# Building the tables ahead of a state-space mixing step in another order, with part of the work moved from VectorE to GpSimd

## The chip, the cores and the metric

The kernel runs on one core of a Trainium2 chip, in a single launch. The metric is device time in microseconds: the median of several executions. Profiles are taken from one execution.

## What is computed

The program is one layer of a tower: a diagonal state-space kernel as token mixer, then attention, then a gated low-rank feed-forward part. The change lies in the first part, which is:

```python
dt = exp(log_dt)                        # H = 256
w = -exp(log_w_real) + 1j * w_imag      # (256, 64)
dtA = w * dt[:, None]
Cm = Cc * (exp(dtA) - 1.0) / w          # Cc: 8 x 256 x 64, complex, the input x
h = 2 * real(einsum('chn,hnl->chl', Cm, exp(dtA[:, :, None] * arange(512))))
# h (8, 256, 512) then goes through
h = h + attention(layernorm(h), w_q, w_k, w_v, w_o)   # 16 heads, 4 kv heads, window 256
h = h + gated_lora_ffn(layernorm(h), ...)             # 8 experts, argmax gate
```

## The kernel before, in words

The 512 positions l are written as l = e0 + 8 e1 + 64 e2 with three digits of 0 to 7. So exp(dtA l) is a product of three small complex factors, one for each level k = 0, 1, 2, and each is a magnitude exp(rho·level) times a cosine and a sine. `mag[:, k]`, `ang[:, k]` and `rnd[:, k]` hold 128 x (128 x 8) values for a level. Level 0 becomes the table v, level 1 the table u, and level 2 the table P (`ptab`). The factor d = (exp(dtA) - 1)/w is multiplied into P; this gives `pa` and its turned copy `pb`.

Four engines build the tables, and each follows its own written-out program with semaphores:

- ScalarE (`trig`, lines 771 to 791): magnitudes of all 24 digits, then for each level sine, absolute value and cosine. Level 0 goes to PSUM (`v_trig`, in `bank_quad`), level 1 to `utab`, level 2 to `ptab`. Between levels 0 and 1 it makes `sin1`, `half` and `cos1`, which d needs. It then splits two weight chunks, and makes from v the rotated v (`vrot`), the edges of b, the copies `lefts`, and `turn_p`, which writes `pb`.
- VectorE: rho (link 16 of its chain, `CH_RHO`), the turns, `reduce_angles` for three levels (a rounding and a subtraction each), the reciprocal of |w|^2, `expm1_parts` with the result `em1`, the u table (`times_mag`, line 1096), d (lines 1101 to 1115), the v table (line 1117), and `p_times_d` (lines 1127 to 1130), which waits for P times its magnitude (`p_mag`). `link` makes each next instruction wait for the one before; instructions without it follow in the pipeline.
- GpSimd: |w|^2 (lines 584 to 589), then P times its magnitude in two halves (line 596), but only after a wait for `d_poles`, and for the second half of the poles three instructions of P times d (605 to 608). Then come the 16 steps of the mixing (`chunk`, lines 570 and 575).
- TensorE: five matmuls to warm up (line 1573) once v is done (`v_done`), then 16 steps of 128 small matmuls (line 1559), each waiting for VectorE (`b_ready`, `g1_ready`), ScalarE (`edges`) and GpSimd (`g2_ready`).

dr, ndr and ndi are slices of `dd` and hold the real part, its negative and the negated imaginary part of d. `d_first` and `d_rest` are copies of them in PSUM. `mw` is exp(log_w_real), kept in `ex`, and `wim` is the imaginary part of w.

Of the kernel before, what the change touches and what calls it, by code (L numbers as in the profile page):

```python
# [21 lines left out]
ALU = mybir.AluOpType  # L22
# [3 lines left out]
P = 128  # L26
# [13 lines left out]
LE = 8  # L40
TYPES = 3
NQ = 16
# [6 lines left out]
ROUND = 1.5 * 2.0 ** 23  # L49
# [27 lines left out]


CH_RHO = 16

GATE, GATE_Z, GATE_KEEP = 15, 7, 11

# [66 lines left out]
def tower(nc, mix_c, mix_s, log_dt, log_wr, w_im, w_qkv, w_o, w_gate, w_gmul, w_upd, centers, slopes, consts, out):  # L149
# [3 lines left out]
    with top:  # L153
        def sem(name):
            return top.enter_context(nc.semaphore(name))

        def sb(name, shape, dt=F32, stack=top):
            return stack.enter_context(nc.sbuf_tensor(name, shape, dt))
# [9 lines left out]
        v_trig = quad[:].rearrange("p k e -> p (k e)").rearrange("p (q r e) -> p q r e", q=NQ, r=2)  # L168
# [22 lines left out]
        vtab = sb("vtab", [P, NQ, 2, 64], F32, mixer)  # L191
        vrot = sb("vrot", [P, NQ, 2, 64], F32, mixer)
        utab = sb("utab", [P, NQ, 2, 64], F32, mixer)
# [6 lines left out]
        mag = sb("mag", [P, TYPES, P, LE], F32, early)  # L200
# [15 lines left out]
        ang = sb("ang", [P, TYPES, P, LE], F32, small)  # L216
        rnd = sb("rnd", [P, TYPES, P, LE], F32, small)
# [6 lines left out]
        wim = sb("wim", [P, P], F32, scratch)  # L224
        rho = sb("rho", [P, P], F32, scratch)
        turn = sb("turn", [P, P], F32, scratch)
        em1 = sb("em1", [P, P], F32, scratch)
        sin1 = sb("sin1", [P, P], F32, scratch)
# [3 lines left out]
        ai = sb("ai", [P, P], F32, scratch)  # L232
        dd = sb("dd", [P, 3, P], F32, scratch)
        ndi, ndr, dr = (dd[:, k, :] for k in range(3))
# [97 lines left out]
        def raw_turn(n):  # L332
# [7 lines left out]
        chain, nrm_parts, nrm_sum = sem("dve_chain"), sem("nrm_parts"), sem("nrm_sum")  # L340
        mag_ready, ang_ready, trig_ready = sem("mag_ready"), sem("angles_ready"), sem("trig_ready")
        abs_done, v_done, u_done, rot_done = sem("abs_done"), sem("v_table"), sem("u_table"), sem("rotated_v")
        wim_in, d_poles, pa_pool, pool_prod, p_mag, p_prod, pa_done, pb_done = (
            sem("wim_in"), sem("d_of_poles"), sem("pa_of_pool"), sem("pool_products"), sem("p_times_mag"), sem("p_products"), sem("pa_ready"), sem("pb_ready"))
        left_ready, t2_done = sem("left_ready"), sem("t2_done")
        b_ready, edges, g1_ready, g2_ready, mixed, evac, xd_out = (
            sem("b_ready"), sem("b_edges"), sem("g1_ready"), sem("g2_ready"), sem("mixed_ready"), sem("evacuated"),
# [208 lines left out]
        def _(pool):  # L556
# [24 lines left out]
            mw = ex[:, 1, :]  # L581
            pool.wait_ge(chain, CH_RHO)
            pool.wait_ge(wim_in, 16)
# [3 lines left out]
            nc.gpsimd.tensor_tensor(nrm[:], nrm[:], wsq[:], ALU.add).then_inc(nrm_parts, 1)  # L587
            pool.wait_ge(nrm_parts, 2)
            nc.gpsimd.tensor_scalar(nrm[:], nrm[:], 0.5, 1.0, ALU.mult, ALU.mult).then_inc(nrm_sum, 1)
            pool.wait_ge(d_poles, 1)  # L590
            pool.wait_ge(trig_ready, 4)
            for k in range(2):
                qs = slice(k * HALF_Q, (k + 1) * HALF_Q)
                m = mag[:, 2].rearrange("p (q h) e -> p q (h e)", q=NQ)[:, qs].unsqueeze(2).to_broadcast(
                    [P, HALF_Q, 2, 64])
                nc.gpsimd.tensor_tensor(ptab[:, qs], ptab[:, qs], m, ALU.mult).then_inc(p_mag, 1)

            def per_pole(t):
                return t[:, HALF_Q * QH8:].rearrange("p (q h) -> p q h", q=HALF_Q).unsqueeze(3).to_broadcast(
                    [P, HALF_Q, QH8, LE])  # L600

            second = slice(HALF_Q, NQ)
            grid = lambda t: t.rearrange("p q (h e) -> p q h e", h=QH8)
            pool.wait_ge(p_mag, 2)
            nc.gpsimd.tensor_tensor(grid(pq[2][:]), grid(ptab[:, second, 0, :]), per_pole(dr), ALU.mult)
            nc.gpsimd.tensor_tensor(grid(pq[3][:]), grid(ptab[:, second, 1, :]), per_pole(ndi), ALU.mult).then_inc(pool_prod, 1)
            pool.wait_ge(pool_prod, 1)
# [142 lines left out]
        def _(act):  # L750
# [11 lines left out]
            levels = [e * LE ** k for k in range(TYPES) for e in range(LE)]  # L762
            act.wait_ge(chain, CH_RHO)
            for k in range(TYPES):
# [111 lines left out]
            def swap(s, parts=range(3), keys=7):  # L876

                for j in parts:
                    view, _, _, _ = rope_view(j)
                    act.wait_ge(proj, s * 3 + (j + 1))  # L880
                    if j == 0 and (not isinstance(s, int) or s):
                        act.wait_ge(kq_rot, s * 3)
                    src = banks[keys][:, 0:S] if j == 0 else banks[j][:].rearrange("p (h s) -> p h s", h=2)
                    nc.scalar.activation(view(sw)[0:64], src[64:128], ACT.Copy)  # L884
                    nc.scalar.activation(view(sw)[64:128], src[0:64], ACT.Copy).then_inc(swapped, 1)  # L885
# [149 lines left out]
        def _(dve):  # L1035
            links = [0]

            def link(ins):

                links[0] += 1  # L1040
                ins.then_inc(chain, 1)
                dve.wait_ge(chain, links[0])

            v = nc.vector

            def expm1_parts(xin, n, raw_in):

                k, r, q, p2 = (t[:].rearrange("p a b -> p (a b)")[:, 0:n] for t in (kk, rr, qq, ki))
                link(v.tensor_scalar(xin, raw_in, -87.0, 88.0, ALU.max, ALU.min))
                link(v.tensor_scalar(k, xin, 1.4426950408889634, ROUND, ALU.mult, ALU.add))  # L1050
                link(v.tensor_scalar(k, k, ROUND, None, ALU.subtract))
                link(v.scalar_tensor_tensor(r, k, -0.693359375, xin, ALU.mult, ALU.add))
                link(v.scalar_tensor_tensor(r, k, 2.12194440e-4, r, ALU.mult, ALU.add))
                link(v.tensor_scalar(q, r, 1.0 / 5040, None, ALU.mult))
                for c in (1.0 / 720, 1.0 / 120, 1.0 / 24, 1.0 / 6, 0.5, 1.0):
                    link(v.scalar_tensor_tensor(q, q, c, r, ALU.add, ALU.mult))
                link(v.tensor_scalar(p2, k, 127.0, 8388608.0, ALU.add, ALU.mult))
                return q, p2.bitcast(F32)
# [3 lines left out]
            q, p2 = expm1_parts(flat, 2 * P, flat)  # L1062
# [3 lines left out]
            dt, mw = ex[:, 0, :], ex[:, 1, :]  # L1066
            link(v.scalar_tensor_tensor(rho[:], mw, -1.0, dt, ALU.mult, ALU.mult))
            assert links[0] == CH_RHO, links
            dve.wait_ge(wim_in, 16)
# [5 lines left out]
            def reduce_angles(k, src):  # L1075

                step = ROUND / LE ** k
                link(v.tensor_scalar(flat(rnd[:, k]), flat(src), step, step, ALU.add, ALU.subtract))
                v.tensor_tensor(flat(ang[:, k]), flat(src), flat(rnd[:, k]), ALU.subtract).then_inc(ang_ready, 1)
                dve.wait_ge(ang_ready, k + 1)  # L1080
# [2 lines left out]
            lv = cst[:, C_L:C_L + LE]  # L1083
            link(v.tensor_tensor(ang[:, 0], turn[:].unsqueeze(2).to_broadcast([P, P, LE]),
                                 lv.unsqueeze(1).to_broadcast([P, P, LE]), ALU.mult))
            for k in range(TYPES):
                reduce_angles(k, ang[:, max(k - 1, 0)])
            dve.wait_ge(nrm_sum, 1)
            link(v.reciprocal(nrm[:], nrm[:]))
            q, p2 = expm1_parts(t0[:], P, rho[:])  # L1090
# [3 lines left out]
            def times_mag(tab, k):  # L1094
                m = mag[:, k].rearrange("p (q h) e -> p q (h e)", q=NQ).unsqueeze(2).to_broadcast([P, NQ, 2, 64])
                return v.tensor_tensor(tab[:], tab[:], m, ALU.mult)

            dve.wait_ge(mag_ready, 3)
            dve.wait_ge(trig_ready, 3)
            times_mag(utab, 1).then_inc(u_done, 1)  # L1100
            link(v.tensor_tensor(t1[:], half[:], half[:], ALU.mult))
            v.scalar_tensor_tensor(ai[:], em1[:], 1.0, sin1[:], ALU.add, ALU.mult)
            link(v.tensor_tensor(ar[:], em1[:], cos1[:], ALU.mult))
            link(v.scalar_tensor_tensor(ar[:], t1[:], -2.0, ar[:], ALU.mult, ALU.add))
            v.tensor_tensor(dr, ai[:], wim[:], ALU.mult)
            v.tensor_tensor(t1[:], ar[:], mw, ALU.mult)
            v.tensor_tensor(ndi, ai[:], mw, ALU.mult)
            link(v.tensor_tensor(t2[:], ar[:], wim[:], ALU.mult))
            v.tensor_tensor(dr, dr, t1[:], ALU.subtract)
            link(v.tensor_tensor(ndi, ndi, t2[:], ALU.add))  # L1110
            v.tensor_tensor(ndi, ndi, nrm[:], ALU.mult)
# [1 line left out]
            link(v.tensor_tensor(dr, dr, nrm[:], ALU.mult))  # L1113
            v.tensor_copy(d_first, dd[:, :, 0:HALF_Q * QH8]).then_inc(d_poles, 1)
            link(v.tensor_copy(d_rest, dd[:, 0:2, HALF_Q * QH8:]))
            m = mag[:, 0].rearrange("p (q h) e -> p q (h e)", q=NQ).unsqueeze(2).to_broadcast([P, NQ, 2, 64])
            v.tensor_tensor(vtab[:], v_trig, m, ALU.mult).then_inc(v_done, 1)

            other = banks[4].rearrange("p (q e) -> p q e", q=HALF_Q)

# [118 lines left out]
            def rope(s, j, keys=7):  # L1239
                view, table, _, _ = rope_view(j)  # L1240
                src = banks[keys][:, 0:S] if j == 0 else banks[j][:].rearrange("p (h s) -> p h s", h=2)
                dve.wait_ge(swapped, s * 3 + (j + 1))
                v.tensor_tensor(view(kq), src, table(cosT), ALU.mult).then_inc(kq_cos, 1)  # L1243
# [701 lines left out]
```

## Time and profile before

| what | value |
|---|---|
| median of 3 runs | 802.74 us (802.38 to 805.21) |
| profiled execution | 801.88 us, its span in the trace 800.0 us |
| TensorE matmul busy | 736.1 us, 92% |
| VectorE busy | 575.0 us, 72% |
| ScalarE busy | 444.9 us, 56% |
| GpSimd busy | 434.4 us, 54% |
| mean granted TensorE clock | 0.994 of full |

The names PE, DVE, ACT, POOL and SP in the profile stand for TensorE, VectorE, ScalarE, GpSimd and the engine that issues most transfers. Times in the trace are microseconds from the start of the span; a line such as L1096 is a line of the kernel. The tables are built in the first 38 us or so and the mixing ends near 98 us. After that come attention and the feed-forward part, in which TensorE is nearly always busy.

### The profile page before, as it was taken

How to read it: one execution, taken by the hardware profiler on the slowest of the kernel's cores; microseconds unless marked ns; L12 is line 12 of the kernel's file. 1: busy time of each engine (PE TensorE's matmuls, PEld its weight loads, DVE VectorE, ACT ScalarE, POOL GpSimd, SP SyncE). 2: the span in 40 equal slices, each digit the busy share in tenths (PEclk: the TensorE clock that was granted, in tenths of full speed). 3: DMA queues.
4: the chain of work that ended last, by engine and by line, in shares of the span. 5: the costliest groups of instructions: out<-in, count | busy, mean ns of one | idle time of the engine just before them, and what ended most of it. 6: DMA issues, size and time to landing. Idle time of an engine off the chain costs nothing.

```text
span 800.0 us, 19498 instructions
## 1 busy us (share of the span) xinstructions
PE 736.1 (92%) x6902; PEld 671.3 (84%) x6902; DVE 575.0 (72%) x1604; ACT 444.9 (56%) x1236; POOL 434.4 (54%) x649
## 2 busy tenths in 40 slices
PE   0277788999999999999999999999999999999996
PEld 0166768999999999999989999999999998989883
DVE  7999877887765666766674565665666678888886
ACT  6735435665555667555674555555575655465431
POOL 1488866644444747544474564444384745665632
PEclk9999999999999999999999999999999999999999
DMA  9023741100010203000011020000020000000403
GB/s 217 6 56 79 178 138 34 54 8 2 7 47 8 67 8 99 7 7 7 7 29 39 1 93 8 7 7 1 8 68 7 29 8 8 7 7 13 100 1 105
DMA packets 38127, 31.59 MB, mean 39 GB/s; under 512 B 23790, under 2 KB 29294, under 8 KB 38070
## 3 DMA queue, kind: packets, MB, share of 16 engines
q1 hardware_dynamic: 37606, 30.25, 14.3%
q8 instruction: 35, 0.57, 0.3%
q10 hardware_dynamic: 464, 0.59, 0.3%
q14 instruction: 22, 0.18, 0.1%
HBM read 20.34 MB, written 10.49 MB: 39 GB/s over the span
## 4 chain that ended last, share of the span: by engine, by line
PE 81%; DVE 7%; POOL 4%; ACT 3%; issue 2%; DMA 1%; DVEq 0%; SPq 0%; ACTq 0%; POOLq 0%
PE bank_quad L1548 17%; PE bank_quad L1547 16%; PE bank_quad L1549 16%; PE bank_pair L1547 4%; PE bank_pair L1548 4%; PE bank_pair L1549 4%; PE bank_quad L1559 2%; PE bank_pair L1736 2%; PE bank_pair L1746 2%; PE bank_quad L1665 2%; PE bank L1746 2%; PE bank L1750 2%; PE bank L1547 2%; PE bank L1548 2%; PE bank L1549 1%
## 5 line engine op out<-in xcount | busy, mean ns | idle before, releaser
L1547 PE MATMUL bank_quad<-xt_hi,w_hi 128*128 128x256 f32 (+1 forms) x568 | 159.5, 281 | 0.0
L1548 PE MATMUL bank_quad<-xt_hi,w_lo 128*128 128x256 f32 (+1 forms) x568 | 158.9, 280 | 0.0
L1549 PE MATMUL bank_quad<-xt_lo,w_hi 128*128 128x256 f32 (+1 forms) x568 | 158.6, 279 | 0.0
L652 POOL TENSOR_TENSOR swap<-swap,cst 128x512 f32<-128x512 f32 (+1 forms) x96 | 105.5, 1110 | 38.4 <-ACT swap L885 38.3
L942 ACT ACTIVATE sm<-sm,mx 128x128 f32<-128x128 f32 (+1 forms) x256 | 113.6, 445 | 20.1 <-DVE mx L1406 20.1
L1249 DVE TENSOR_TENSOR kq<-kq,swap 128x512 f32<-128x512 f32 (+1 forms) x96 | 89.9, 957 | 25.9 <-POOL swap L652 24.8
L1547 PEld LDWEIGHTS bank_quad<-xt_hi,w_hi 128*128 128x128 f32 x568 | 106.8, 188 | 0.0
L1548 PEld LDWEIGHTS bank_quad<-xt_hi,w_lo 128*128 128x128 f32 x568 | 106.7, 188 | 0.0
L1549 PEld LDWEIGHTS bank_quad<-xt_lo,w_hi 128*128 128x128 f32 x568 | 106.3, 187 | 0.0
L692 POOL TENSOR_SCALAR sm<-sm,rinv 128x128 f32<-128x128 f32 (+1 forms) x256 | 103.9, 418 | 0.1
L954 ACT ACTIVATE ot_hi<-bank_quad 128x512 fp32r<-128x512 f32 x64 | 37.8, 597 | 118.4 <-PE bank_quad L1549 118.4
L419 POOL TENSOR_TENSOR spare<-cst 1x1 f32<-1x1 f32 x70 | 14.2, 203 | 159.2 <-DVE rinv L1418 151.0
L657 POOL TENSOR_TENSOR kq_lo<-kq,kq_hi 128x256 fp32r<-128x256 f32 x93 | 67.4, 751 | 51.4 <-ACT kq_hi L893 51.4
L1243 DVE TENSOR_TENSOR kq<-bank_quad,cst 128x512 f32<-128x512 f32 (+1 forms) x78 | 50.1, 642 | 59.1 <-ACT swap L885 58.7
L884 ACT ACTIVATE swap<-bank_quad 64x512 f32<-64x512 f32 (+1 forms) x78 | 43.4, 556 | 77.9 <-PE bank_quad L1549 77.0
L1397 DVE TENSOR_TENSOR ot_lo<-bank_quad,ot_hi 128x512 fp32r<-128x512 f32 x64 | 43.4, 678 | 23.5 <-ACT ot_hi L954 23.4
L1547 PE MATMUL bank_quad<-wo_hi,ot_hi 128*128 128x512 f32 x132 | 55.0, 416 | 0.4 <-DVE ot_lo L1397 0.4
L1549 PE MATMUL bank_quad<-wo_lo,ot_hi 128*128 128x512 f32 x132 | 51.9, 393 | 0.0
L1548 PE MATMUL bank_quad<-wo_hi,ot_lo 128*128 128x512 f32 x132 | 51.5, 390 | 0.0
L1549 PE MATMUL bank_pair<-wo_lo,ot_hi 128*128 128x512 f32 x124 | 48.2, 389 | 0.0
L1547 PE MATMUL bank_pair<-wo_hi,ot_hi 128*128 128x512 f32 x124 | 48.2, 389 | 0.0
L1548 PE MATMUL bank_pair<-wo_hi,ot_lo 128*128 128x512 f32 x124 | 48.2, 389 | 0.0
(347 smaller groups left out, 2133.9 us busy)
## 6 DMA issues: line engine op xcount, KB each, us to landing
mixed<-st SPq DMA_DIRECT2D x32, 128.0 KB, 2.0
x<-mixed SPq DMA_DIRECT2D x32, 128.0 KB, 3.0
out<-x SPq DMA_DIRECT2D x28, 128.0 KB, 2.3
raw<-in_w_qkv SPq DMA_DIRECT2D x8, 384.0 KB, 3.7
raw<-in_w_o SPq DMA_DIRECT2D x10, 256.0 KB, 2.8
norm_mem<-in_w_qkv SPq DMA_DIRECT2D x6, 384.0 KB, 4.2
later_v<-v_next SPq DMA_DIRECT2D x16, 128.0 KB, 1.7
v_next<-later_v SPq DMA_DIRECT2D x16, 128.0 KB, 2.0
```

The source lines that it names most:

```text
L652: nc.gpsimd.tensor_tensor(view(sw), view(sw), table(sinT), ALU.mult).then_inc(rot_sin, 1)
L657: nc.gpsimd.tensor_tensor(flat(kl), part(kq), flat(kh).bitcast(F32), ALU.subtract).then_inc(kq_lo, 1)
L692: last = nc.gpsimd.tensor_scalar(sm[:, j, cols], sm[:, j, cols], rinv[:, 2 * j + t:2 * j + t + 1], 1.0, ALU.mult, ALU.mult)
L884: nc.scalar.activation(view(sw)[0:64], src[64:128], ACT.Copy)
L942: last = nc.scalar.activation(sm[:, j, cols], sm[:, j, cols], ACT.Exp, scale=-1.0, bias=mx[:, n:n + 1], accum_out=rsum[:, n:n + 1])
L954: nc.scalar.activation(by_rows(oth, j), natural(banks[first_bank + j]), ACT.Copy).then_inc(ot_hi, 1)
L1243: v.tensor_tensor(view(kq), src, table(cosT), ALU.mult).then_inc(kq_cos, 1)
L1249: v.tensor_tensor(view(kq), view(kq), view(sw), ALU.add).then_inc(kq_rot, 1)
L1397: v.tensor_tensor(by_rows(otl, j), natural(banks[first_bank + j]), by_rows(oth, j).bitcast(F32), ALU.subtract).then_inc(ot_lo, 1)
L1547: mmul(dst, lh, rh, start=start and k == 0, stop=False, skip_group_check=True)
L1548: mmul(dst, ll, rh, start=False, stop=False, skip_group_check=True)
L1549: last = mmul(dst, lh, rl, start=False, stop=stop and k == n - 1, skip_group_check=True)
```

## The change

It does four things.

1. The angles of level 2 are no longer made by VectorE from those of level 1. GpSimd makes them from level 0, with two tensor_scalar instructions (add, then subtract, a large constant) and a subtraction over 1024 columns.
2. The imaginary part of exp(dtA) - 1 (`ai`) and its products with `wim` and `mw` are made by GpSimd, in four instructions of 128 columns, after `em1` and `cos1`. VectorE then waits for them (`d_parts`).
3. VectorE's order changes: real part of d, v table, rest of d, u table. Before it was u table, d, v table.
4. GpSimd scales P when its sines are there. It waits for d only before its products of P with d.

```diff
+CH_EM1 = 37
 # GpSimd
             nc.gpsimd.tensor_scalar(nrm[:], nrm[:], 0.5, 1.0, ALU.mult, ALU.mult).then_inc(nrm_sum, 1)
-            pool.wait_ge(d_poles, 1)
+            flat_level = lambda t: t.rearrange("p h e -> p (h e)")
+            step_two = ROUND / LE ** 2
+            pool.wait_ge(ang_ready, 1)
+            nc.gpsimd.tensor_scalar(flat_level(rnd[:, 2]), flat_level(ang[:, 0]), step_two, 1.0, ALU.add,
+                                    ALU.mult).then_inc(level_two, 1)
+            pool.wait_ge(level_two, 1)
+            nc.gpsimd.tensor_scalar(flat_level(rnd[:, 2]), flat_level(rnd[:, 2]), -step_two, 1.0, ALU.add,
+                                    ALU.mult).then_inc(level_two, 1)
+            pool.wait_ge(level_two, 2)
+            pool.wait_ge(ang_ready, 2)
+            nc.gpsimd.tensor_tensor(flat_level(ang[:, 2]), flat_level(ang[:, 0]), flat_level(rnd[:, 2]),
+                                    ALU.subtract).then_inc(ang_ready, 1)
+
+            pool.wait_ge(chain, CH_EM1)
+            pool.wait_ge(trig_ready, 2)
+            nc.gpsimd.tensor_scalar(ai[:], em1[:], 1.0, 1.0, ALU.add, ALU.mult).then_inc(d_half, 1)
+            pool.wait_ge(d_half, 1)
+            nc.gpsimd.tensor_tensor(ai[:], ai[:], sin1[:], ALU.mult).then_inc(d_half, 1)
+            pool.wait_ge(d_half, 2)
+            nc.gpsimd.tensor_tensor(dr, ai[:], wim[:], ALU.mult)
+            nc.gpsimd.tensor_tensor(ndi, ai[:], mw, ALU.mult).then_inc(d_parts, 1)
             pool.wait_ge(trig_ready, 4)
+            pool.wait_ge(mag_ready, 3)
...
             pool.wait_ge(p_mag, 2)
+            pool.wait_ge(d_poles, 1)
 # VectorE
-            for k in range(TYPES):
-                reduce_angles(k, ang[:, max(k - 1, 0)])
+            for k in range(2):
+                reduce_angles(k, ang[:, 0])
...
-            dve.wait_ge(mag_ready, 3)
-            dve.wait_ge(trig_ready, 3)
-            times_mag(utab, 1).then_inc(u_done, 1)
+            assert links[0] == CH_EM1, links
+            dve.wait_ge(trig_ready, 2)
             link(v.tensor_tensor(t1[:], half[:], half[:], ALU.mult))
-            v.scalar_tensor_tensor(ai[:], em1[:], 1.0, sin1[:], ALU.add, ALU.mult)
             link(v.tensor_tensor(ar[:], em1[:], cos1[:], ALU.mult))
             link(v.scalar_tensor_tensor(ar[:], t1[:], -2.0, ar[:], ALU.mult, ALU.add))
-            v.tensor_tensor(dr, ai[:], wim[:], ALU.mult)
             v.tensor_tensor(t1[:], ar[:], mw, ALU.mult)
-            v.tensor_tensor(ndi, ai[:], mw, ALU.mult)
             link(v.tensor_tensor(t2[:], ar[:], wim[:], ALU.mult))
+            dve.wait_ge(mag_ready, 1)
+            m = mag[:, 0].rearrange("p (q h) e -> p q (h e)", q=NQ).unsqueeze(2).to_broadcast([P, NQ, 2, 64])
+            v.tensor_tensor(vtab[:], v_trig, m, ALU.mult).then_inc(v_done, 1)
+            dve.wait_ge(d_parts, 1)
             v.tensor_tensor(dr, dr, t1[:], ALU.subtract)
             link(v.tensor_tensor(ndi, ndi, t2[:], ALU.add))
...
             link(v.tensor_copy(d_rest, dd[:, 0:2, HALF_Q * QH8:]))
-            m = mag[:, 0].rearrange("p (q h) e -> p q (h e)", q=NQ).unsqueeze(2).to_broadcast([P, NQ, 2, 64])
-            v.tensor_tensor(vtab[:], v_trig, m, ALU.mult).then_inc(v_done, 1)
+            dve.wait_ge(mag_ready, 2)
+            dve.wait_ge(trig_ready, 3)
+            times_mag(utab, 1).then_inc(u_done, 1)
```

## Rows read from the trace of the kernel before

**Rows 1.** The page: span, and busy time by engine.
```profile
span 800.0 us, 19498 instructions
PE 736.1 (92%) x6902; PEld 671.3 (84%) x6902; DVE 575.0 (72%) x1604; ACT 444.9 (56%) x1236; POOL 434.4 (54%) x649
```
**Rows 2.** Chain that ended last, 10 to 46 us: start, length, what.
```profile
31.25 0.37 DVE bank_pair L1114
...
44.75 1.04 POOL g L575
```
**Rows 3.** Timeline of ACT: start, length, instruction, count, idle time before and releaser.
```profile
27.48 1.15 ACT L779 ACTIVATE ptab<-rnd,cst 128x1024 f32<-128x1024 f32 x1
...
34.17 1.06 ACT L792 ACTIVATE vrot<-vtab 128x1024 f32<-128x1024 f32 x1 [3.86 <-DVE vtab L1117]
```
**Rows 4.** Timeline of DVE, 17 to 46 us.
```profile
17.25 0.69 DVE L1078 TENSOR_SCALAR rnd<-ang 128x1024 f32<-128x1024 f32 x1
17.97 1.23 DVE L1079 TENSOR_TENSOR ang<-ang,rnd 128x1024 f32<-128x1024 f32 x1
...
24.46 0.29 DVE L1092 SCALAR_TENSOR_TENSOR em<-ki,em 128x128 f32<-128x128 f32 x1
25.68 2.29 DVE L1096 TENSOR_TENSOR utab<-utab,mag 128x2048 f32<-128x2048 f32 x1 [0.93 <-ACT utab L779]
...
31.84 2.29 DVE L1117 TENSOR_TENSOR vtab<-bank_quad,mag 128x2048 f32<-128x2048 f32 x1
34.08 0.69 DVE L1127 TENSOR_TENSOR pq<-ptab,bank_pair 128x512 f32<-128x512 f32 x1
...
37.46 0.69 DVE L1130 TENSOR_TENSOR pa<-bank_pair,pq 128x512 f32<-128x512 f32 x1
...
45.36 0.98 DVE L1153 TENSOR_TENSOR bt<-bank,vtab 128x784 f32<-128x784 f32 x1 [0.27 <-PE bank_quad L1559]
```
**Rows 5.** Timeline of POOL, 12 to 40 us.
```profile
12.10 1.32 POOL L587 TENSOR_TENSOR nrm<-nrm,wsq 128x128 f32<-128x128 f32 x1
...
31.70 4.67 POOL L596 TENSOR_TENSOR ptab<-ptab,mag 128x1024 f32<-128x1024 f32 x2 [17.58 <-DVE bank_pair L1114]
...
39.86 1.96 POOL L570 TENSOR_TENSOR g<-cim,pb 128x1024 f32<-128x1024 f32 x1
```
**Rows 6.** Groups of POOL by shape: count, busy us, mean ns, idle before.
```profile
L692 POOL TENSOR_SCALAR sm<-sm,rinv 128x128 f32<-128x128 f32 x128 | 46.8, 365 | 0.1
...
L681 POOL TENSOR_SCALAR norm_mem<-norm_mem,norm 128x512 f32<-128x512 f32 x10 | 6.8, 684 | 0.0
```
**Rows 7.** Timelines of DVE and POOL around 99, 152 and 469 us, one summary line.
```profile
99.71 2.08 POOL L565 TENSOR_TENSOR w_lo<-raw,w_hi 128x896 fp32r<-128x896 f32 x1
99.78 2.29 DVE L1258 TENSOR_SCALAR norm_mem<-x,norm 128x512 f32<-128x512 f32 x1 [2.38 <-POOL norm L627]
...
106.55 0.55 DVE L1258 TENSOR_SCALAR norm_mem<-x,norm 128x512 f32<-128x512 f32 x1 [0.94 <-POOL norm L639]
...
152.47 2.73 DVE L1249 TENSOR_TENSOR kq<-kq,swap 128x256 f32<-128x256 f32 x1 [1.89 <-POOL swap L652]
...
469.63 1.51 DVE L1249 TENSOR_TENSOR kq<-kq,swap 128x256 f32<-128x256 f32 x1 [0.76 <-POOL swap L652]
...
L1249 DVE TENSOR_TENSOR kq<-kq,swap x96: 415/692/2735, 115.3 to 748.6; 128x512 f32<-128x512 f32 x64, 128x256 f32<-128x256 f32 x32
```
**Rows 8.** Timeline of PE, 34 to 61 us, and the busy time of one stretch.
```profile
34.28 7.34 PE L1573 MATMUL bank_quad<-cst 128*128 128x512 f32 x10 [34.28 <-DVE vtab L1117]
42.98 2.10 PE L1559 MATMUL bank_quad<-bt,g 64*64 64x64 f32 x128 [1.36 <-POOL g L575]
...
56.92 3.64 PE L1559 MATMUL bank_quad<-bt,g 64*64 64x64 f32 x128
...
57.00:60.50 3.50, 3.50 (x129) 3.39 (x129) 3.47 (x6) 0.88 (x4) 2.44 (x2) 0.51 0.36 75
```
**Rows 9.** Busy time of PE, PEld, DVE, ACT, POOL, 80 to 90 us.
```profile
80.00:90.00 10.00, 7.56 (x428) 7.11 (x422) 10.00 (x13) 4.50 (x18) 9.14 (x7) 1.00 0.76 183
```

More of the change, by code:

```diff
@@ L342, in tower @@
         abs_done, v_done, u_done, rot_done = sem("abs_done"), sem("v_table"), sem("u_table"), sem("rotated_v")
-        wim_in, d_poles, pa_pool, pool_prod, p_mag, p_prod, pa_done, pb_done = (
-            sem("wim_in"), sem("d_of_poles"), sem("pa_of_pool"), sem("pool_products"), sem("p_times_mag"), sem("p_products"), sem("pa_ready"), sem("pb_ready"))
+        d_half, d_parts, level_two, wim_in, d_poles, pa_pool, pool_prod, p_mag, p_prod, pa_done, pb_done = (
+            sem("d_half"), sem("d_parts"), sem("level_two"), sem("wim_in"), sem("d_of_poles"), sem("pa_of_pool"), sem("pool_products"), sem("p_times_mag"), sem("p_products"), sem("pa_ready"), sem("pb_ready"))
         left_ready, t2_done = sem("left_ready"), sem("t2_done")
```

## The prediction

> **What bounds the kernel now.** I read the page first. TensorE is busy for 92% of an 800.0 us span [rows 1], but that average says nothing of the first 50 us, where the change lies. So the chain that ended last comes next, cut to the stretch before the mixing [rows 2]. It runs over ScalarE to the last sine of u, then VectorE (the u table, then d, whose first copy ends at 31.61), then GpSimd from 31.70: two halves of P, two products and their sum, the operands of the first two mixing steps, the last of which ends at 45.79. The timelines of the three engines give the slack. ScalarE has all sines of P at 28.63 (27.48 + 1.15). After two weight splits it waits 3.86 us for the v table, from 30.31 to 34.17 [rows 3]. VectorE sits 0.93 us before the u table, and from there to 45 us has no idle time [rows 4]. GpSimd finished the norm early and has stood idle since, until d's first copy came, 17.58 us by its own row [rows 5]. Later in the mixing VectorE is full: 10.00 of 10.00 us between 80 and 90 [rows 9]. So the whole front of the kernel is serial, each microsecond there moves the end by about one, and the question is when the mixing can start.
>
> **What it would be without contention.** Removed from VectorE: one 1024-column rounding and subtraction (17.25 to 19.20, 1.98 us with the gaps [rows 4]) and three small products of about 0.2 us each in the pipeline. GpSimd no longer waits for d: P's sines are there at 28.63, so its first half could start at 28.7 instead of 31.70, 3.0 us earlier. VectorE would then have, from em1 at 22.8: five instructions of d (1.5), v table (2.3) to 26.6, the rest of d with its copies (1.9) to 28.5, u table (2.3) to 30.7. The first half of P ends at 31.05, so the six products and sums of P with d (34.08 to 38.15 before, 4.07 us [rows 4]) start 3.0 earlier too. ScalarE's two weight splits end at 30.3 and the rotated v by 32.4, which is in time. The bound of the gain is therefore 3.0 us: ScalarE's own chain up to 28.63 is untouched. The new waits for magnitudes cost nothing: ScalarE makes them all before its first sine.
>
> **Why I do not take it.** The moved work makes GpSimd and VectorE read SBUF at once, which before they hardly did in this stretch. The trace shows what that does [rows 7]. VectorE's subtract-and-scale of 128x512 takes 0.55 us alone, and 2.29 us when issued just after a GpSimd split of 2.08. Its kq addition of 128x256 (0.42 alone, by the same line's minimum) takes 1.51 beside one GpSimd instruction, and 2.73 where two GpSimd instructions follow each other without a gap. So the later one waits for all of the earlier one, less about 0.13 us. GpSimd pays as well: its addition for the norm took 1.32 us, beside VectorE's angles, for some 0.45 of work [rows 5]. But the v table, which has PSUM as one operand, took 2.29 us beside the scaling of P, no more than the u table did alone [rows 4].
>
> Step by step, with these prices. **Third level on GpSimd.** Two scalings of 1024 columns are not in the trace: 0.365 at 128 and 0.684 at 512 [rows 6] give 0.83 ns per column, so 1.11 each (bounds 0.9 and 1.4); the subtraction is as long as a half of P, 2.34 [rows 5] (bound below 2.0). VectorE begins its rounding of level 1 at 15.27 (17.25 less 1.98), so the first angle is ready at 15.23. GpSimd's first scaling waits for VectorE's rounding until about 15.8 and ends at 16.9; VectorE's subtraction (due 15.99) waits for it to 16.8 and ends at 18.0; GpSimd's second ends at 19.0, its subtraction runs 19.2 to 21.5 and holds up VectorE's short instructions of expm1 for 2.1 us. Angle level two is on time (ScalarE wants it at 25.5), but em1 ends at 25.7, not at 24.75: 1.98 saved, 2.9 paid. **d's imaginary products.** GpSimd's four 128-column instructions (about 0.4 each, 1.9 with hand-overs) run beside the five of VectorE, both ending near 28. **v table** 27.9 to 30.2, no contention, 3.9 us earlier than before; that only lets ScalarE and the five warm-up matmuls start earlier. **P against d.** GpSimd starts P at 28.7 and its halves follow each other without a gap, to 33.35. Queued behind the v table on VectorE is dr, two SBUF operands, at 30.2: it waits for one half or for both, and in either case the next linked one comes only after 33.2. d's first copy ends at 34.8 instead of 31.61 [rows 2]. **u table against the products.** GpSimd, now waiting for d as before, takes 34.9 to 37.0 for its two products. The u table, due at 35.1 and with both operands in SBUF, starts at 36.9 if the two hold it up together, 35.7 if it gets in between. It ends at 39.2 or 38.0. Behind it in VectorE's queue stand the six products, whose start was 34.08: now 39.1 or 37.9. Their sums gate ScalarE's copies to pb (1.2 us, as 38.15 to 39.33 before), and these gate GpSimd's first g: 44.4 or 43.3 against 39.86, so +4.6 or +3.5 us. In short, u came before d and ran beside an idle GpSimd; now it comes last, beside a busy one, and P's half that was saved waits for it.
>
> The Trainium skill (SBUF — State Buffer, "Who interferes with whom") says that the shared port pair is an exclusive lock held for a whole instruction, and that VectorE with at most one SBUF input stays out of it. By that rule taken per instruction a waiting engine enters between two, +3.5; by the 2.73 us row it can wait for both, +4.6.
>
> **TensorE's clock.** The first mixing step took 2.10 us at full clock right after the warm-up; the one at 56.92 took 3.64 with the granted clock at 0.51, that is 1.2 instead of 2.4 GHz, after a stretch in which TensorE had been half idle [rows 8]. The warm-up still lasts 7.34 us but starts with the v table, at 30.3, and ends at 37.6. The first step comes at 46.5 to 47.5: some 9 us idle instead of 1.36. I take it to run at 1.2 GHz: +1.54. VectorE waits for its end before its third step (45.36 [rows 4], with 0.27 of idle there, so slack is small): of 1.54 I keep 1.4. Against it stand 0.4 us of wait behind the slow step at 56.92, which may fall elsewhere. Net +1.0. Bounds: 0 (clock stays up) to +1.8 (second step slow too).
>
> Sum: (3.5 to 4.6) + 1.0, middle +5.1. The profiled execution took 801.88 (span 800.0), 0.9 below the median of the runs, so I expect about 807.0 in a profile and 802.74 + 5.1 = **807.8 us** as the median. Everything behind the mixing hangs on it by data and moves along; ScalarE and GpSimd wait for no transfer in this stretch. I call 0.5% (4 us) the least that a measurement of this kernel can tell.
>
> **Rivals.**
> *Clean gain (other side).* The price of running side by side is small, by overlap falling in gaps: P starts at 28.7 and nothing else is late. For it: idle GpSimd, the chain [rows 2]. Against it: [rows 7]. 3.0 us gained, of which the slow first step (now after some 6 us of idle) takes 1.1: 800.9; with the clock up 799.7. It decides from the point at which d's last link is through before P starts at 28.7; em1 would have to end by 22.8.
> *Short VectorE instructions pass ahead of a waiting GpSimd.* Then the angle subtraction waits until em1 and d's real part are through (25.6), P starts at 29.6, dr at 31.8, u runs 33.7 to 36.0 ahead of P's second half, first g at 41.9: +2.0, with the clock +3.0, 805.8. Against it: the addition for the norm [rows 5] got in between VectorE's angles and the rounding, which was linked and so left a gap of 0.03 us.
> *A double block before the v table.* If em1 slips past 26.3, d's fifth instruction is still queued when P starts, waits for both halves, and the v table comes after 33.3: +7.7 at the first g, 811. It needs only 0.6 us more than I found, but the slower prices of the bounds at once.
>
> **Chances.** Forecast 0.62 (own range 806.0 to 809.5), passing ahead 0.17, clean gain 0.15, double block 0.06. Slower by over 0.5% (over 806.75): four fifths of the forecast, 0.50, and the double block: 0.56. Faster by over 0.5% (under 798.7) needs more than the bound of 3.0 us: 0.03, for what I overlook. The rest, 0.41, is within 0.5%. The range 801.5 to 809.8 leaves out most of the clean gain (0.12) and the double block with a bit of the forecast (0.08).
>
> **What the profile after would show.** Right: VectorE's angle subtraction and one of the expm1 instructions about 1 and 2 us longer than before, dr or its neighbour stretched by 2 to 3 us around 30 to 33, a u table of 3 to 4 us near 35 to 39, first g of GpSimd near 44, a first mixing step of 3.6 us at clock 0.5. Wrong: u and P each at their old length while they overlap, and the first g near 37; or em1 near 22.8. The clock term is wrong if the first step takes 2.1 us. If the mixing starts late as said and the end does not, the mixing had slack that I deny.

## The result and the profile after

The changed kernel takes 806.77 us in the median (805.95 to 808.34, 6 runs), the kernel before beside it 803.66 (802.38 to 805.21, 6 runs). The ratio is 1.0042, its 95% interval 1.0031 to 1.0054: slower, by a little under the 0.5% that I had called the least to be told. Run once more, beside later experiments, it took 806.76 against 802.76, ratio 1.0051 (1.0038 to 1.0065). The profiled execution took 806.25, with a span of 804.4.

The page first: TensorE and ScalarE do the same work in the same time, VectorE and GpSimd are busier, VectorE with five instructions fewer [rows 1].
```profile
span 804.4 us, 19505 instructions
PE 736.3 (92%) x6902; PEld 672.1 (84%) x6902; DVE 579.6 (72%) x1599; ACT 445.4 (55%) x1236; POOL 444.2 (55%) x656
```
The timeline of VectorE (columns as in [rows 4]):
```profile
15.80 1.94 DVE L1102 TENSOR_TENSOR ang<-ang,rnd 128x1024 f32<-128x1024 f32 x1
...
18.76 2.39 DVE L1072 TENSOR_SCALAR t<-rho 128x128 f32<-128x128 f32 x1
...
25.17 0.29 DVE L1115 SCALAR_TENSOR_TENSOR em<-ki,em 128x128 f32<-128x128 f32 x1
...
26.15 0.48 DVE L1125 SCALAR_TENSOR_TENSOR ar<-t,ar 128x128 f32<-128x128 f32 x1
26.67 0.50 DVE L1126 TENSOR_TENSOR t<-ar,ex 128x128 f32<-128x128 f32 x1
27.09 0.54 DVE L1127 TENSOR_TENSOR t<-ar,wim 128x128 f32<-128x128 f32 x1
27.66 2.29 DVE L1130 TENSOR_TENSOR vtab<-bank_quad,mag 128x2048 f32<-128x2048 f32 x1
29.87 1.15 DVE L1132 TENSOR_TENSOR dd<-dd,t 128x128 f32<-128x128 f32 x1
30.94 2.43 DVE L1133 TENSOR_TENSOR dd<-dd,t 128x128 f32<-128x128 f32 x1
...
34.13 0.36 DVE L1137 COPY bank_pair<-dd 128x192 f32<-128x192 f32 x1
...
34.72 3.14 DVE L1119 TENSOR_TENSOR utab<-utab,mag 128x2048 f32<-128x2048 f32 x1
37.79 0.67 DVE L1151 TENSOR_TENSOR pq<-ptab,bank_pair 128x512 f32<-128x512 f32 x1
...
50.27 0.97 DVE L1177 TENSOR_TENSOR bt<-bank,vtab 128x784 f32<-128x784 f32 x1 [1.49 <-PE bank_quad L1583]
```
The timeline of GpSimd in the same stretch:
```profile
15.13 1.54 POOL L594 TENSOR_SCALAR rnd<-ang 128x1024 f32<-128x1024 f32 x1 [1.19 <-DVE ang L1102]
16.75 1.89 POOL L597 TENSOR_SCALAR rnd<-rnd 128x1024 f32<-128x1024 f32 x1
18.73 2.35 POOL L601 TENSOR_TENSOR ang<-ang,rnd 128x1024 f32<-128x1024 f32 x1
...
28.50 4.72 POOL L618 TENSOR_TENSOR ptab<-ptab,mag 128x1024 f32<-128x1024 f32 x2 [1.02 <-ACT ptab L802]
34.64 1.07 POOL L628 TENSOR_TENSOR pq<-ptab,dd 128x512 f32<-128x512 f32 x1 [1.42 <-DVE bank_pair L1137]
35.67 3.12 POOL L629 TENSOR_TENSOR pq<-ptab,dd 128x512 f32<-128x512 f32 x1
...
43.17 1.95 POOL L571 TENSOR_TENSOR g<-cim,pb 128x1024 f32<-128x1024 f32 x1 [3.02 <-ACT pb L831]
```
Read the two beside each other. At five places where both engines have all their operands in SBUF, one of them is long by 0.7 us or more. The angle subtraction takes 1.94 us (1.23 before). The first instruction of expm1 ends at 21.15, just after GpSimd's subtraction ends at 21.08: 2.39 for 0.23 of work, with a single input. dr (L1132) ends at 31.02, some 0.15 after the middle of P's two halves, and ndi (L1133) at 33.37, just after the second. The u table waits for GpSimd's first product, and the second product then waits for the u table: that product ends at 38.79 and takes 3.12 instead of 1.07. The v table, one operand in PSUM, keeps its 2.29 while GpSimd starts on P. So the first g is issued at 43.17 instead of 39.86 [rows 5]. This trace begins 0.2 us later in the program than that of before (rho is at 10.60, not 10.78), so the first g is 3.5 us late.

The timeline of TensorE:
```profile
30.10 6.93 PE L1597 MATMUL bank_quad<-cst 128*128 128x512 f32 x10 [30.10 <-DVE vtab L1130]
46.29 6.53 PE L1583 MATMUL bank_quad<-bt,g 64*64 64x64 f32 x256 [9.26 <-POOL g L576]
```
And the busy time of one stretch (columns as in [rows 9]):
```profile
46.00:50.00 4.00, 3.71 (x140) 3.74 (x144) 2.74 (x4) 0.03 (x1) 3.08 (x3) 0.50 0.02 6
```
In the chain that ended last the first step stands as (start, length, what):
```profile
46.29 3.73 PE bank_quad L1583 x128
```
After 9.26 us of idle the first mixing step runs at half the clock (0.50, that is 1.2 GHz) and takes 3.73 us instead of 2.10.

### The profile page after: what moved, and what is told of

It is laid out like the page before. It is cut to its first block, busy times and chain, and to the rows that moved or that the text cites. A ratio compares the mean times of both kernels' runs of the same rounds, so it can differ in the third digit from the quotient of the medians.

```text
span 804.4 us, 19505 instructions
## 1 busy us (share of the span) xinstructions
PE 736.3 (92%) x6902; PEld 672.1 (84%) x6902; DVE 579.6 (72%) x1599; ACT 445.4 (55%) x1236; POOL 444.2 (55%) x656
## 4 chain that ended last, share of the span: by engine, by line
PE 80%; DVE 11%; issue 3%; POOL 2%; ACT 1%; DMA 1%; DVEq 0%; SPq 0%; POOLq 0%
PE bank_quad L1571 16%; PE bank_quad L1572 16%; PE bank_quad L1573 16%; PE bank_pair L1571 4%; PE bank_pair L1572 4%; PE bank_pair L1573 4%; PE bank_pair L1760 2%; PE bank_pair L1770 2%; PE bank_quad L1689 2%; PE bank L1770 2%; PE bank L1774 2%; PE bank L1571 2%; PE bank L1572 2%; PE bank L1573 1%; DVE bank_pair L1180 1%
## 5 line engine op out<-in xcount | busy, mean ns | idle before, releaser
L1273 DVE TENSOR_TENSOR kq<-kq,swap 128x512 f32<-128x512 f32 (+1 forms) x96 | 89.9, 957 | 25.7 <-POOL swap L675 24.7
```

The costliest lines, as they stand in the source:

```text
L1273: v.tensor_tensor(view(kq), view(kq), view(sw), ALU.add).then_inc(kq_rot, 1)
```

## The experiments

The theory: VectorE's instructions with SBUF operands alone, and those with two of them above all, hold GpSimd up and are held up by it, and this is the whole loss. What the two engines exclude each other from is called the port below; the runs show the waiting, not the port itself. The rival on the size: the slow first step, not contention, carries the rest, about 1 us. In each line below, "ratio" is against the kernel before on the same chip.

**1. The first step at full clock.** TensorE's warm-up waits for the u table too.
```diff
+            pe.wait_ge(u_done, 1)      # ahead of the five warm-up matmuls
```


> The changed kernel, but the five warm-up matmuls of TensorE wait for the u table (37.9 us) and no longer for the v table (30.1). Theory (TensorE idles 9 us between warm-up and first mixing step, so the first step runs at 1.2 GHz, and VectorE waits for its end): the first step takes 2.1 us instead of 3.7, VectorE's third step starts at about 48.8 instead of 50.3, and the median is 1.4 us under the changed kernel's 806.8, so about 805.4. Rival (the mixing absorbs a slow first step, because VectorE or GpSimd sets its pace anyway): the first step is fast, the end stays at 806.8.

Measured: 806.56 us (805.41 to 807.75), ratio 1.0041 (1.0026 to 1.0057). TensorE and VectorE:
```profile
38.29 5.92 PE L1597 MATMUL bank_quad<-cst 128*128 128x512 f32 x10 [38.29 <-DVE utab L1119]
46.58 2.63 PE L1583 MATMUL bank_quad<-bt,g 64*64 64x64 f32 x128 [2.37 <-POOL g L576]
...
49.47 0.97 DVE L1177 TENSOR_TENSOR bt<-bank,vtab 128x784 f32<-128x784 f32 x1 [0.41 <-PE bank_quad L1583]
```
The first step took 2.63 (the clock fell in its course) and VectorE's third step came 0.8 us earlier (1.1 from the same start), but the median hardly moved: 806.56 against 806.77, where 805.4 had been expected. My term of 1.0 us is not in the median, which is known to about 1.3 us.

**2. The u table off the port.** Magnitudes of level 1 in PSUM; nothing else is changed.
```diff
+        last_two = top.enter_context(nc.psum_tensor("bank_last", [P, 2, 512], F32))
+        mag_one = last_two[:].rearrange("p r (h e) -> p (r h) e", e=LE)
-                    last = nc.scalar.activation(mag[:, k, :, e], rho[:], ACT.Exp, scale=float(levels[k * LE + e]))
+                    last = nc.scalar.activation(mag_one[:, :, e] if k == 1 else mag[:, k, :, e], rho[:], ACT.Exp, scale=float(levels[k * LE + e]))
-                m = mag[:, k].rearrange(...)
+                m = (mag_one if k == 1 else mag[:, k]).rearrange(...)
```


> The changed kernel, but ScalarE writes the magnitudes of level 1 to PSUM, so that VectorE's u table has only one operand in SBUF. Theory (VectorE with two SBUF operands and GpSimd exclude one another for whole instructions): the u table takes 2.3 us instead of 3.14, GpSimd's second product 1.1 instead of 3.12, the products of P with d start 0.8 us earlier, median 806.0. Rival (the two only share SBUF's bandwidth in general, or a queue delay stretched them): both keep their lengths wherever the operand lies, 806.8.

Measured: 805.54 us (12 runs), ratio 1.0031 (1.0020 to 1.0041). VectorE and GpSimd:
```profile
34.62 2.29 DVE L1121 TENSOR_TENSOR utab<-utab,bank_last 128x2048 f32<-128x2048 f32 x1
...
35.57 1.07 POOL L631 TENSOR_TENSOR pq<-ptab,dd 128x512 f32<-128x512 f32 x1
...
42.21 1.95 POOL L573 TENSOR_TENSOR g<-cim,pb 128x1024 f32<-128x1024 f32 x1 [4.22 <-ACT pb L833]
```
The u table took 2.29 instead of 3.14 and GpSimd's second product 1.07 instead of 3.12, side by side. The first g came 1.0 earlier and the median is 1.2 lower; the intervals of the two ratios still overlap, so it is the durations that show the cause, not the median.

**3. Nearly everything off the port.** Also expm1's intermediates, those of d's real part, and 1/|w|^2 in PSUM. Of VectorE's instructions between the angles and the u table, em1 times cos1 alone still has SBUF operands only; the angle subtraction keeps them too.
```diff
+        x_ps, t2_ps, nrm_ps, r_ps, k_ps, q_ps = (tmp[:, a:a + P] for a in (0, 128, 256, 384, 512, 896))
-            v.tensor_tensor(dr, dr, t1[:], ALU.subtract)
-            link(v.tensor_tensor(ndi, ndi, t2[:], ALU.add))
-            v.tensor_tensor(ndi, ndi, nrm[:], ALU.mult)
+            v.tensor_tensor(dr, dr, x_ps, ALU.subtract)
+            link(v.tensor_tensor(ndi, ndi, t2_ps, ALU.add))
+            v.tensor_tensor(ndi, ndi, nrm_ps, ALU.mult)
 ...
```


> The changed kernel, but nearly every VectorE instruction between the angles and the u table has an operand or its input in PSUM (temporaries of expm1 and of d, the reciprocal, magnitudes of level 1), with the same order and the same work on GpSimd. Left in SBUF are the angles and two or three instructions of 0.3 us. Theory (the port took the gain): em1 ends near 23.5 instead of 25.5, P's halves and d run side by side, u ends near 31.6, GpSimd's first g starts near 37 instead of 43.2; TensorE's first step stays slow (1.2 GHz), so against the kernel before -2.7 + 1.3: about 802.2. Rival (the order itself is bad: GpSimd's slower instructions and the hand-overs lengthen the path): the first g stays after 41 and the median at 805 or above.

Measured: 800.00 us (798.86 to 801.84), ratio 0.9958 (0.9941 to 0.9974). VectorE, then GpSimd:
```profile
19.68 0.29 DVE L1117 TENSOR_SCALAR bank_pair<-rho 128x128 f32<-128x128 f32 x1
...
28.49 0.28 DVE L1147 TENSOR_TENSOR dd<-dd,bank_pair 128x128 f32<-128x128 f32 x1
...
29.52 0.36 DVE L1151 COPY bank_pair<-dd 128x192 f32<-128x192 f32 x1
...
30.11 2.29 DVE L1133 TENSOR_TENSOR utab<-utab,bank_last 128x2048 f32<-128x2048 f32 x1
...
19.64 2.35 POOL L604 TENSOR_TENSOR ang<-ang,rnd 128x1024 f32<-128x1024 f32 x1
...
29.21 4.70 POOL L621 TENSOR_TENSOR ptab<-ptab,mag 128x1024 f32<-128x1024 f32 x2 [2.71 <-ACT ptab L805]
...
37.71 1.95 POOL L574 TENSOR_TENSOR g<-cim,pb 128x1024 f32<-128x1024 f32 x1 [0.26 <-ACT pb L834]
```
The first instruction of expm1 takes 0.29 beside GpSimd's subtraction, where it took 2.39, and the u table keeps 2.29 beside P. em1 ends 1.8 us earlier than after the change, from the same start, so dr and ndi are through at 28.77, before P starts at 29.21: they are short here because they come first, and experiment 9 shows them beside P. All of the loss is gone and 3.0 us more: the same order of work now beats both kernels. I had expected 802.2, with 1.3 us for a slow first step. That step was slow (3.65 us), and the median does not have the term.

**4. Experiment 3 with the later warm-up of experiment 1.**
```diff
+            pe.wait_ge(u_done, 1)      # on top of experiment 3
```


> The one without shared SBUF operands, and the warm-up of TensorE waiting for the u table. Theory: the gain of 2.7 us at the first g reaches the end undiminished, median about 800.9, under the kernel before by 2.5 to 3. Rival (the clock term is nothing): the same as the run without the later warm-up.

Measured: 799.96 us (799.04 to 800.73), ratio 0.9953 (0.9938 to 0.9968). TensorE:
```profile
39.98 2.10 PE L1597 MATMUL bank_quad<-bt,g 64*64 64x64 f32 x128 [1.09 <-POOL g L579]
...
52.21 1.03 PE L1597 MATMUL bank_quad<-bt,g 64*64 64x64 f32 x53 [1.49 <-issue]
```
The first step is at full clock, and the time is that of experiment 3. A wait of 1.49 us for nothing that the profile shows stands in the fourth step, as in the trace of before; after the change and in experiment 3 it is gone or down to 0.28. It looks as if the slow step used time that TensorE lost anyway; more of that behind experiment 9.

**5. P waits for d again.**
```diff
+            pool.wait_ge(d_poles, 1)   # ahead of P times its magnitude, as in the kernel before
```


> The changed kernel with one part undone: GpSimd again waits for d before it scales P. Theory (P beside d on the shared port is what holds d up): the rest of d takes 1.3 us again and its first copy ends near 31.6 instead of 34.5; P's first half then starts at 31.7 and the u table waits for it, ending near 36.2 instead of 37.9; the first g comes near 42.1 instead of 43.2, so the median falls by about 1.1, to about 805.5. Rival (the start of P is what counts, contention is second): P and with it the first g come up to 3 us later than in the changed kernel, 807 to 810.

Measured: 805.42 us (9 runs), ratio 1.0021 (1.0011 to 1.0031). VectorE and GpSimd:
```profile
30.07 0.28 DVE L1133 TENSOR_TENSOR dd<-dd,t 128x128 f32<-128x128 f32 x1
...
31.91 4.35 DVE L1120 TENSOR_TENSOR utab<-utab,mag 128x2048 f32<-128x2048 f32 x1
...
31.76 6.71 POOL L619 TENSOR_TENSOR ptab<-ptab,mag 128x1024 f32<-128x1024 f32 x2 [4.08 <-DVE bank_pair L1138]
...
41.95 1.96 POOL L571 TENSOR_TENSOR g<-cim,pb 128x1024 f32<-128x1024 f32 x1
```
With the wait restored, d is short again and the u table and P's second half pay instead (4.35, and 6.71 for both halves). Starting P later, by 3.1 us from the same start, makes the kernel faster by 1.3 in the median. The first g is still 2.1 us later than in the kernel before: the u table, which now comes last, waits for P.

**6. Level 2 back on VectorE** (all else as changed), run twice.
```diff
-            for k in range(2):         # and GpSimd's three instructions for level 2 left out
+            for k in range(TYPES):
```


> The changed kernel with one part undone: VectorE makes the angles of level 2 again (from level 0), GpSimd does not. em1 comes 0.9 us earlier (24.5), because VectorE pays 1.98 for the work and saves 0.71 and 2.16 of waiting. Theory (d is released only when P's second half is through, whatever em1 does): dr and its neighbour wait until 33.2 as before, the first g stays at 43.2, the median within 0.4 of the changed kernel's. Rival (em1's slip is the cost): the first g moves with em1, -0.9.

> The changed kernel with the angles of level 2 made by VectorE, once more: its first g stood where theory put it, but its median was 1.4 us above the changed kernel's, with a mean granted clock of 0.985 in most executions. Theory (more stretches at 1.2 GHz in those executions, on another chip, nothing of the edit): beside the changed kernel on one chip the two differ by less than 0.8 us. Rival (the edit costs something behind the first g): again 1.2 us or more above the changed kernel.

> The changed kernel unaltered, for a comparison on one chip with the next. Ratio to the kernel before 1.0042 as in the result (1.003 to 1.0055).

Measured: 808.17 us (ratio 1.0062, 1.0049 to 1.0075), then 807.38 (1.0055, 1.0042 to 1.0069) beside the changed kernel's 806.76 (1.0051). VectorE and GpSimd of the first:
```profile
29.39 2.05 DVE L1121 TENSOR_TENSOR dd<-dd,t 128x128 f32<-128x128 f32 x1
31.37 2.43 DVE L1122 TENSOR_TENSOR dd<-dd,t 128x128 f32<-128x128 f32 x1
...
43.60 1.95 POOL L571 TENSOR_TENSOR g<-cim,pb 128x1024 f32<-128x1024 f32 x1 [3.03 <-ACT pb L820]
```
dr came 0.5 us earlier (0.9 from the same start) and took 0.9 longer, up to the same middle of P. With its later trace start (0.4), the first g is where it was. The first run's 1.4 us beyond the changed kernel was a miss of the theory, which the second brought down to 0.6, with intervals that overlap. So where P blocks d, level 2 on GpSimd moves the first g neither way. Whether it costs anything further on stays open: both traces of this version have a mean granted clock of 0.83 between 140 and 150 us, both of the changed kernel 1.00.

**7. P ahead of d alone, in the kernel before.**
```diff
-            pool.wait_ge(d_poles, 1)
             pool.wait_ge(trig_ready, 4)
+            pool.wait_ge(mag_ready, 3)
 ...
+            pool.wait_ge(d_poles, 1)   # ahead of the products of P with d
```


> The kernel before with one part of the change alone: GpSimd scales P as soon as its sines are there and waits for d only before its products. Theory: the u table is through before P starts (28.5), but d's products on VectorE, with both operands in SBUF, wait for both halves of P, so d's copy comes near 35.7 instead of 31.6, the v table at 38.4, the first g near 43.7: slower than before by about 4, some 807. Rival (as the change intended: P off the path of d): P ends 3 us earlier, first g near 39.5, the same time as before or 0.4 less.

Measured: 806.86 us (5 runs), ratio 1.0045 (1.0032 to 1.0058). GpSimd, then VectorE:
```profile
28.59 4.69 POOL L596 TENSOR_TENSOR ptab<-ptab,mag 128x1024 f32<-128x1024 f32 x2 [14.58 <-ACT ptab L780]
...
28.62 2.46 DVE L1105 SCALAR_TENSOR_TENSOR ar<-t,ar 128x128 f32<-128x128 f32 x1
31.12 2.31 DVE L1106 TENSOR_TENSOR dd<-ai,wim 128x128 f32<-128x128 f32 x1
...
43.51 1.95 POOL L570 TENSOR_TENSOR g<-cim,pb 128x1024 f32<-128x1024 f32 x1 [4.23 <-ACT pb L809]
```
One moved wait, without the rest of the change, makes a loss of the same size, by two instructions of 0.29 us that take 2.46 and 2.31. Its first mixing step is at full clock (2.09 us), and although it starts 3.8 us late, the gaps of the kernel before are there, 0.48 us in the third step and 1.22 in the fourth:
```profile
58.59 1.03 PE L1560 MATMUL bank_quad<-bt,g 64*64 64x64 f32 x53 [1.22 <-issue]
```

**8. The control: the PSUM operands of experiment 3 in the kernel before.**
```diff
-            v.tensor_tensor(dr, dr, t1[:], ALU.subtract)
+            v.tensor_tensor(dr, dr, x_ps, ALU.subtract)      # and the others of experiments 2 and 3
```


> A control: the kernel before, in its own order, with the same temporaries, the reciprocal and the magnitudes of level 1 in PSUM as in the run without shared operands. Theory (in the kernel before nothing of this ran beside GpSimd, so there is nothing to free): within 0.4 us of the kernel before. Rival (PSUM operands are faster in themselves, and the gain of 3 us had nothing to do with the new order): about 3 us under the kernel before.

Measured: 803.23 us against 803.23, ratio 1.0000 (0.9992 to 1.0009). PSUM operands are worth nothing by themselves. A short instruction even takes 0.29 with them where it took 0.23, and em1 ends 0.3 us later, which VectorE's idle time before the u table takes up (0.93 before, 0.39 here). In experiment 3 they are worth 6.8 us because GpSimd runs beside them.

**9. Experiment 3 with level 2 back on VectorE.**
```diff
-            for k in range(2):         # on top of experiment 3, as in experiment 6
+            for k in range(TYPES):
```


> The version without shared SBUF operands, but with the angles of level 2 made by VectorE. Theory (without contention VectorE's own work sets d and u, and it gets 1.98 us of level 2 back while losing the 0.7 us it waited at the angles): em1, u and the first g all about 1.0 to 1.2 us later than in the version without shared operands, median 801.0 against 800.0. Rival (ScalarE's and GpSimd's chain over P sets the first g): no difference.

Measured: 802.21 us (11 runs), ratio 0.9993 (0.9984 to 1.0002). VectorE, then GpSimd:
```profile
28.74 0.28 DVE L1135 TENSOR_TENSOR dd<-dd,bank_pair 128x128 f32<-128x128 f32 x1
28.94 0.28 DVE L1136 TENSOR_TENSOR dd<-dd,bank_pair 128x128 f32<-128x128 f32 x1
...
28.37 4.69 POOL L610 TENSOR_TENSOR ptab<-ptab,mag 128x1024 f32<-128x1024 f32 x2 [1.43 <-ACT ptab L794]
```
Here dr and ndi run beside P, each with one operand in PSUM, and take 0.28 us where they took 1.15 and 2.43. The first g, at 38.15, is 1.3 us behind that of experiment 3 when both are set to the same start of the trace. In profiles the last matmul comes 0.9 later; the median is 2.2 behind, on another chip, and 1.2 above the 801.0 expected. The intervals of the two ratios do not overlap, so once the port is free, level 2 on GpSimd is worth its place; the size, 0.9 by the traces and 2.8 by the difference of the ratios (0.0035), is not settled. Nor is it explained why a first g 1.6 us earlier than in the kernel before leaves the median within its noise.

**What became of the first step.** For each profiled execution I took the start of TensorE's n-th matmul, from ScalarE's first exponential on, less the same of the kernel before (us):

| kernel | first step at | first step | third step | just after the mixing | last matmul |
|---|---|---|---|---|---|
| changed | half clock | +3.5 | +5.0 | +4.4 | +4.7 |
| changed, second trace | mostly half | +3.5 | +4.7 | +4.6 | +4.5 |
| 1, later warm-up | mostly full | +3.5 | +3.9 | +3.5 | +3.7 |
| 7, P alone | full | +3.8 | +3.8 | +4.6 | +5.6 |
| 3, off the port | mostly half | -2.9 | -1.5 | -2.1 | -0.9 |
| 4, and later warm-up | full | -2.9 | -2.9 | -1.8 | -0.9 |
| 8, the control | full | -0.2 | -0.2 | +0.7 | +0.6 |
| 9, level 2 back | mostly half | -1.6 | -0.6 | -1.1 | 0.0 |

The changed kernel loses 1.5 us by its third step and has 0.9 of it left after the mixing (1.2 and 1.1 in its second trace). But of the kernels whose first step was at full clock all three grow by 0.8 to 1.1 over the mixing as well, the control among them, whose median is that of the kernel before. The trace of before was a quick execution (801.88, medians of 802.74 to 803.66), which would account for most of that 0.9. The two pairs that differ in the warm-up alone disagree: after the mixing experiment 1 is 0.9 us ahead of the changed kernel, but in an execution that was the quickest of its six (805.41); experiment 4 is 0.3 behind experiment 3.

Part of the slow step is caught up at one place, the gap ("issue") within the fourth step. That step's last 53 matmuls begin 12.0 to 12.2 us after the start of the first step in the four traces with a full-clock first step (before, 4, 7 and 8), and 12.3 to 12.7 in the eight with a slow one. The matmuls just ahead of them begin at 10.5 in the former and 11.6 to 12.1 in the latter. So most of the 1.1 to 1.6 us by which a slow first step is longer is taken out of a gap that is there otherwise, whether the mixing starts early or late. Experiment 1, with 11.5, lies outside both, and what the gap waits for is not known.

## Why the prediction was right, and where it was off

The mechanism was right: GpSimd and VectorE wait for one another, and the first g comes 3.5 us late. The number is nearer than it should be. Forecast was 802.74 + 5.1 = 807.8, measured 806.77, but the kernel before stood at 803.66 beside it. The rise was 3.1 us (4.0 when run again), so 0.9 of the miss was hidden by luck.

- **Third level on GpSimd**: right in kind and place. Forecast: subtraction of VectorE done at 18.0, GpSimd's at 21.5, em1 at 25.7. Measured (0.2 us of trace start apart): 17.74, 21.08, 25.46. The two scalings took 1.54 and 1.89 rather than 1.11, since part of each is waiting: each ends 0.9 after the VectorE instruction beside it.
- **d's imaginary products**: 1.94 us from 25.55, as said. Unforeseen was that they stretch three VectorE instructions beside them to 0.48, 0.50 and 0.54, about 0.2 each.
- **P against d**: right. dr got in between the halves, which the forecast had left open, and ndi waited for the second; d's first copy ended at 34.49 (forecast 34.8).
- **u against the products**: the earlier of my two branches, u in between: end at 37.86 (forecast 38.0 or 39.2), the six products from 37.79, first g 3.5 us late. I had taken the middle of 3.5 and 4.6, half a microsecond too much. The Trainium skill's rule of a lock for each instruction (SBUF — State Buffer, "Who interferes with whom") gave +3.5, and the trace agrees (3.5); so do experiments 2 and 9 with its exception for at most one SBUF input (2.29 and 0.28 us beside GpSimd). The Trainium skill's section limits the exception to instructions outside VectorE's two-port modes, which the prediction left unsaid. The first instruction of expm1 has one SBUF input and took 2.39 us; no run shows the mode that it ran in. The 2.73 us row of [rows 7], where one waiter seems to have sat out two instructions, is not explained; none of the runs here bears on it.
- **TensorE's clock**: the mis-sized term. The first step ran at 1.2 GHz and took 3.73 us, VectorE's third step moved by 4.91, both as said. But the +1.0 at the end is not seen in a median: experiments 1 and 4 gave the first step its clock back (1 for most of it) for 0.2 and 0.0 us. Each of these medians is known to about 1.3 us, so a part of the 1.0 may be there; the trace of experiment 1 has 0.9 of it, that of experiment 4 none. I had denied that the mixing has slack, on the 0.27 us before VectorE's third step alone. It has some for a slow first step: the gaps that the profile lists under "issue", which stood in steps three and four of before and shrink when the first step is long.
- **The sum**: 3.5 of contention and -0.4 to +0.5 for all else, against 4.05 + 1.0. The two runs of the changed kernel gave 3.1 and 4.0 us by their medians. The forecast of 807.0 for a profile stands against 806.25. That each microsecond of the front moves the end by about one held for experiment 3 (2.9 and 3.0), not for experiment 9 (1.6 and 0.6).
- **The rivals**: passing ahead did not happen (the subtraction of level 2 was never held up till em1), nor the double block. The clean gain's mechanism was absent. Its size, 3.0 us, was that of experiment 3, where most of VectorE's instructions stay off the port.

## What to carry to other kernels

Before work goes to an idle GpSimd, write beside it what VectorE does in that time and count the SBUF operands: a 0.3 us instruction with two of them costs what is left of GpSimd's, and one with a single SBUF input that writes to SBUF did too (0.23 became 2.39). A wait that looks useless may be what keeps such an instruction out of the way (experiment 7 lost 3.6 us by moving one). The cure here was not to undo the change but to put one operand of each VectorE instruction in PSUM, which cost nothing measurable itself (experiment 8). And compare a shift with a control before putting a microsecond down to a cause: single executions of one kernel differ by that much (802.38 to 805.21 us in the kernel before).

## What the hardware showed that I had not expected

- GpSimd waits as well as VectorE: its 1.07 us product took 3.12 beside a VectorE instruction of 2.29, and P's two halves took 6.71 instead of 4.7.
- A first step 1.1 to 1.6 us longer at half clock cost 0.2 and 0.0 us of median (experiments 1 and 4, each known to about 1.3 us).
- The "issue" gaps early in the mixing go with the length of the first step and not with the time at which it starts. They are 0.48 and 1.22 or 1.49 us in all four traces with a full-clock first step, one of them 3.8 us late; in the others the first is gone and the second is 0 to 0.81. What they are stayed open.
- Further stretches at 1.2 GHz fall in some traces and not in others. One begins near 143 us in experiment 7 (0.50 from 144 to 146) and goes with the 1.0 us by which its last matmul is later than its mixing. Experiments 5 and 6 have one there too, the kernel before and the changed kernel do not.
- Not every instruction of VectorE is held up: the reciprocal (one operand) took its 0.95 us beside GpSimd's second scaling.
